# Moving the block loads and weight stores of an output projection from SyncE's queue to ScalarE's

## The reference

```
x = x + attention1(xn) + feed_forward1(xn)
# the end of attention1
out = out.transpose(0, 2, 1, 3).reshape(b, s, NH * HD)     # 2048 wide
return out @ o_w.T                                          # 2048 -> 512
# the start of feed_forward1: weights in packed 4-bit floats
nib = w[:, :, None] >> shifts & jnp.uint32(15)
vals = _FP4_LUT[nib.astype(jnp.int32)].reshape(out_f, in_p * 8)
s_full = jnp.repeat(s, group_size, axis=1)
return vals * s_full
```

## Time and profile before

| | |
|---|---|
| median of 3 runs | 2429.59 us |
| the profiled execution | 2425.01 us |
| its span, first to last instruction | 2422.9 us |
| mean granted TensorE clock | 0.96 |
| PE, PEld, DVE busy | 88%, 61%, 62% |
| ACT, POOL busy | 37%, 21% |
| DMA moved in the span | 242.99 MB |

### The profile page before, as it was taken

How to read it: one execution, slowest core, us unless ns; L and a number is a source line. 1 busy time by engine, 2 the same in 40 slices (tenths; PEclk the granted TensorE clock), 3 DMA queues, 4 the chain that set the end, 5 groups by cost and what they waited for, 6 DMA issues and landing times. The chain is left out here.

```text
span 2422.9 us, 53839 instructions
## 1 busy us (share of the span) xinstructions
PE 2127.0 (88%) x22256; PEld 1484.4 (61%) x22256; DVE 1499.6 (62%) x2380; ACT 891.2 (37%) x1858; POOL 511.2 (21%) x419
## 2 busy tenths in 40 slices
PE   4899969999996999868888988888986788799997
PEld 3677747777775788724444444444444666687776
DVE  4544323333324455468999889988894786177776
ACT  3322123222222300035656556565563232134443
POOL 0110112122220145401111111111112455221111
PEclk9999989999998999979999999999998898899999
DMA  4121144000005633233443334333342866541100
GB/s 153 71 88 36 71 154 144 17 26 17 9 0 212 198 126 122 106 83 83 104 109 90 98 81 112 102 89 98 81 119 85 262 210 194 178 144 52 53 1 35
DMA packets 183984, 242.99 MB, mean 100 GB/s; under 512 B 37744, under 2 KB 110768, under 8 KB 181072
## 3 DMA queue, kind: packets, MB, share of 16 engines
q1 hardware_dynamic: 182896, 239.59, 32.1%
q10 hardware_dynamic: 864, 0.21, 0.0%
HBM read 156.82 MB, written 82.90 MB: 99 GB/s over the span
## 5 line engine op out<-in xcount | busy, mean ns | idle before, releaser
L1479 ACT ACTIVATE a_prob<-ps,a_nmax 128x256 f32<-128x256 f32 (+7 forms) x512 | 377.4, 739 | 349.1 <-DVE a_nmax L1507 212.2
L1592 PE MATMUL ps<-a_kt,a_q 64*128 64x512 f32 (+5 forms) x1536 | 378.0, 533 | 88.0 <-ACT a_prob L1479 64.7
L1507 DVE TENSOR_REDUCE a_nmax<-ps 128x1 f32<-128x1024 f32 (+3 forms) x256 | 256.3, 1001 | 74.1 <-PE ps L1592 72.7
L1524 DVE STREAM_TRANSPOSE a_pt_long<-a_prob 128x512 f32<-128x512 f32 (+3 forms) x512 | 278.3, 582 | 0.0
L1592 PEld LDWEIGHTS ps<-a_kt,a_q 64*128 64x128 f32 x1536 | 142.0, 191 | 186.4 <-ACT a_prob L1479 117.1
L1606 PE MATMUL ps<-a_pt_long,a_v 32*64 32x256 f32 (+3 forms) x7808 | 228.0, 344 | 1.8 <-DVE a_pt_long L1524 0.2
L1991 DVE SCALAR_TENSOR_TENSOR f_part<-ps,f_gu_scale,f_part 128x512 f32<-128x512 f32 x264 | 184.7, 745 | 65.0 <-PE ps L2039 51.7
L1606 PEld LDWEIGHTS ps<-a_pt_long,a_v 32*64 32x64 f32 x7808 | 153.6, 131 | 103.4 <-issue 75.6
L1559 POOL TENSOR_TENSOR a_o<-a_left 128x256 f32<-128x256 f32 x128 | 90.4, 729 | 594.9 <-ACT a_left L1489 594.9
L2039 PE MATMUL ps<-f_xt_hi,f_gu 128*128 128x512 f32 x352 | 142.3, 404 | 22.1 <-DMA f_wd_lo<-scratch_wd 12.6
L843 POOL TENSOR_TENSOR f_hT_lo<-f_h,f_hT_hi 128x512 fp32r<-128x512 f32 x64 | 82.0, 1293 | 325.0 <-ACT f_hT_hi L826 325.0
(11 more groups left out here) (225 smaller groups left out, 4518.5 us busy)
## 6 DMA issues: line engine op xcount, KB each, us to landing
a_q<-scratch_QT SPq DMA_DIRECT2D x512, 64.0 KB, 2.1
scratch_QT<-k_qo SPq DMA_DIRECT2D x64, 256.0 KB, 2.3
a_v<-scratch_V SPq DMA_DIRECT2D x64, 256.0 KB, 4.7
scratch_OT<-a_o SPq DMA_DIRECT2D x32, 512.0 KB, 3.3
o_of<-scratch_OT SPq DMA_DIRECT2D x32, 512.0 KB, 5.5
o_packed<-in_packed SPq DMA_DIRECT2D x11, 768.0 KB, 6.8
f_xt_hi<-scratch_xt SPq DMA_DIRECT2D x8, 1024.0 KB, 7.3
f_xt_lo<-scratch_xt SPq DMA_DIRECT2D x8, 1024.0 KB, 9.1
```

Of the source, the lines that this page charges most:

```text
L1479: last = nc.scalar.activation(prob[:, n % PRING, s].rearrange("p (a w) -> p a w", w=w), SC[n % 2][:, a, 0:w], ACT.Exp, bias=nmax[:, n % 4, ...
L1507: nc.vector.tensor_reduce(nmax[:, n % 4, 0:1], SC[n % 2][:, :, 0:width(0, t)], AX.XY, ALU.max, negate=True).then_inc(maxed, 1)
L1524: last = nc.vector.transpose(pt[hf][:, lo:hi, h, t - FIRST[hf], :], src.rearrange("p (j k) -> p j k", k=32))
L1592: last = pe.matmul(sc[:, a, 0:w], q[r, slot, heads[a * hf], :], kt[r, b, keys], start=not masked, stop=True, skip_group_check=True)
```

## The change

SP keeps the loads of `stage`, `of`, `xsum` and the shift table. The block loads and all stores are issued by ACT. ACT loads the first two blocks ahead of its loop. At `STORE_AT[m]`, which is one step later than before for ACT and for POOL, it converts block m, issues the load of block m+2, stores the low down weights of block m-1 and stores the converted parts of block m. The load's wait for unpacking goes, since `convert(m)` has waited for the same block already.

```diff
-        LOAD_AT = [0, 1] + [OPS * (m - 1) // SHARE + 1 for m in range(2, NBK)]
-        STORE_AT = [OPS * (m + 1) // SHARE + 1 for m in range(NBK)]
+        STORE_AT = [OPS * (m + 1) // SHARE + 2 for m in range(NBK)]
...
             @block.sync
             def _(sp):
-                def load_block(m):
-                    if m >= 2:
-                        sp.wait_ge(unpacked, OPS * (m - 1))
-                    sp.dma_start(packed[:, m % 2, :], d["packed"][m, :, :].unsqueeze(1).broadcast_to([P // 8, 8, WC])
-                                 ).then_inc(p_in[m % 2], 16)
-                    sp.dma_start(scale[:, m % 2, :], d["down_scale"][m, :].partition_broadcast(P)
-                                 ).then_inc(p_in[m % 2], 16)
-
-                def store_block(m):
-                    sp.wait_ge(converted, 2 * m + 2)
-                    sp.dma_start(d["gu"][m], gu[:, m % 2, :].bitcast(F32)).then_inc(w_stored[m % 2], 16)
-                    sp.dma_start(d["wd"][0, m], wd[0][:, m % 2, :].bitcast(F32)).then_inc(w_stored[m % 2], 16)
-                    sp.wait_ge(down_low, m + 1)
-                    sp.dma_start(d["wd"][1, m], wd[1][:, m % 2, :].bitcast(F32)).then_inc(w_stored[m % 2], 16)
...
-                        for m in block_at(n):
-                            load_block(m)
...
-                    for m in range(NBK):
-                        if n == STORE_AT[m]:
-                            store_block(m)
...
             @block.scalar
             def _(act):
+                def load_block(m):
+                    act.dma_start(packed[:, m % 2, :], d["packed"][m, :, :].unsqueeze(1).broadcast_to([P // 8, 8, WC])
+                                  ).then_inc(p_in[m % 2], 16)
+                    act.dma_start(scale[:, m % 2, :], d["down_scale"][m, :].partition_broadcast(P)
+                                  ).then_inc(p_in[m % 2], 16)
+
+                def store_converted(m):
+                    act.wait_ge(converted, 2 * m + 2)
+                    act.dma_start(d["gu"][m], gu[:, m % 2, :].bitcast(F32)).then_inc(w_stored[m % 2], 16)
+                    act.dma_start(d["wd"][0, m], wd[0][:, m % 2, :].bitcast(F32)).then_inc(w_stored[m % 2], 16)
+
+                def store_low(m):
+                    act.wait_ge(down_low, m + 1)
+                    act.dma_start(d["wd"][1, m], wd[1][:, m % 2, :].bitcast(F32)).then_inc(w_stored[m % 2], 16)
...
+                for m in range(2):
+                    load_block(m)
                 for n in range(NSTEP + 1):
...
                         if n == STORE_AT[m]:
                             convert(m)
+                            if m + 2 < NBK:
+                                load_block(m + 2)
+                            if m:
+                                store_low(m - 1)
+                            store_converted(m)
+                store_low(NBK - 1)
```

More of the change, by code:

```diff
@@ L1689, in finished @@
             return n + 1 + (n + 1) // NK * (TT - 1)
-        def block_at(n):
-            return [m for m in range(NBK) if n == LOAD_AT[m]]
         SHARE = 3
-        LOAD_AT = [0, 1] + [OPS * (m - 1) // SHARE + 1 for m in range(2, NBK)]
-        STORE_AT = [OPS * (m + 1) // SHARE + 1 for m in range(NBK)]
+        STORE_AT = [OPS * (m + 1) // SHARE + 2 for m in range(NBK)]
         with nc.Block() as block:
```

## The result

The changed kernel took 2406.45 us (median of 4 runs, 2400.58 to 2408.3) beside 2430.39 us for the kernel before (4 runs, 2426.3 to 2431.31). The ratio is 0.9897, with a 95% interval of 0.988 to 0.9915: 24 us less, 1.0%. Timed once more beside other variants it took 2404.88 us, ratio 0.99 (0.9883 to 0.9916). The forecast was 2406.6.

The account below looks back on a forecast made before the run. SP's DMA queue, 131 us in semaphore waits with slice loads behind it, was taken to leave holes in PE, VectorE being next. Second half 13.8 plus first half 9.2 gave 23 us: 2406.6 us, range 2391 to 2426.

Parts of the forecast that it names:

- the rivals' times: Only second half gains 2415.6 us (chance 0.22); everything fits 2394 (0.15); no change 2429.6 (0.10); slower 2440 (0.08).
- SP's order: SP's DMA queue: block loads and stores leave it, and 131 us of waits that held up slice loads go.
- SP's issues and the later step: SP's saved issuing, 25 us, only in the no-change rival (0.10); conversion one step later: no gain by itself.
- Second half, 13.8 us: Tokens n = 16 to 31: PE sets the pace, 101.8 becomes 87.0 us, gain 14.8, less 1 for ACT's convert waits.
- First half, 13.1 less 3.9: Tokens n = 0 to 15: PE starts step 15 13.1 us earlier, less 3.9 for crowded DMA engines; net 9.2.
- The new wait for packed blocks: First half, VectorE waits for blocks 2, 4 and 5, now issued by ACT: 3.6 + 3.8 + 2.1 = 9.5 us.
- The adds, taken as free: VectorE's eight adds at the half, 5.0 us, counted ahead of unpacking block 7, with no wait of PE for them.
- The start: Stage start: packed(0) beside of(0) may start PE up to 2.5 us later; taken as 0, since VectorE ends the half.
- ACT's issues: Block loads and stores on ACT, up to 30 us over 11 blocks: just hidden in PE's 5.44 us step; taken as 0.
- the 3 us to spare: Second half, convert(7) on ACT: oT_lo(21) ends at 24.2 us into the half, PE needs it at 27.2.
- DMA share: First half: the DMA engines' share rises from 0.79 to 0.85 or more; 0.88 by the count.
- The upper bound: Best case, packed at 5.7 us to landing and no crowding: first half gains 22, second 14.8, 37 us in all.

Follow-up runs that it names:

- the four tests here: Changed kernel with only loads on ACT: 2425.74 us; only stores on ACT: 2412.5; all DMAs on ACT, SP's waits kept: 2425.19; kernel before with later step: 2443.27.
- the fourth: Kernel before with only conversion, low part and stores one step later, everything on SP: 2443.27 us, ratio 1.0066.

## Why the prediction was right

The mechanism was right: SP's waits, with the slices queued behind them, held PE, and with them gone VectorE bounds the first half. None of the rivals' times came. That the total agreed so closely (24 us measured, 23 forecast) is in part luck. In the traces the two halves gained 8.1 and 12.0 us, 20.1 in all; the other 4 us of the medians lie in no stage that the traces single out. And inside the first half errors of opposite sign cancelled. The terms, one by one:

- *SP's order.* Right, and shown: the waits put back, without the DMAs, cost 19 of the 24 us.
- *SP's issues and the later step, both taken as nothing.* They were not: 18 us for the DMAs' move with the waits kept, and 13 us lost by the later step while all is in SP's order. The sum holds because these two nearly cancel.
- *Second half, 13.8 us.* In the traces PE's part from step 16 on fell from 101.8 to 89.8: 12.0. The run is free of holes, as forecast. The 2 us that are missing are its slow beginning. Behind the wait for the adds step 16 took 7.98 us (1990.09 to 1998.07) and not 5.44, with a granted clock of 0.56 between 1990 and 1996 us, and I had put no restart there.
- *First half, 13.1 less 3.9.* PE reached step 16 8.1 us earlier, counted from the stage's start, against 9.2. Near as that is, every part was off. At step 15 PE was 13.0 us earlier (1979.74 - 1867.73 against 1990.9 - 1865.87), 3.8 more than forecast. The new wait for packed blocks, put at 9.5 us and 3.9 more for crowding, was 2.8: 10.6 too much. VectorE's operations, left at their old durations, took 6.1 us more: its last wo_lo ended 108.2 us after its first one began, of which 8.2 was waiting, so 100.0 us for the work that took 118.4 - 5.0 - 19.5 = 93.9 before. The rest of the difference, 0.6, is a later start.
- *The adds, taken as free.* They were not: step 15's three operations took 9.7 us and not 5, so the adds began late and PE stood 4.6 us. With it the 13.0 us at step 15 became the 8.1 at step 16.
- *Why the packed wait was small.* I counted oT_hi and both conversions, 2.8 us, as lying ahead of the load's issue, because they stand ahead of it in ACT's order. The trace shows that they don't (below). The other part is that VectorE's steps were 6.8 us long, and so it came to the block later than my 6.1 us said.
- *The start.* PE's first matmul came 3.5 us later in the stage, more than my bound of 2.5. Nothing speaks against taking 0 for its effect: made 3.1 us earlier again, the stage was 212.8 us as before, and with 2.5 operations a step 202.2 against 201.5. But in both VectorE's loads moved too, so it isn't shown by itself.
- *ACT's issues.* Hidden, as forecast: PE doesn't wait for ACT or POOL behind step 16. ACT does stand at the conversions of blocks 6 to 10, 24.1 us in all and at most 8.1 (block 6), and the 3 us to spare held.
- *DMA share.* Forecast at 0.85 or more, 0.82 measured; it was no bound. Between 1900 and 1940 us, where the residual is loaded too, it is 1.01, and VectorE's single wait for `scale` falls in there.
- *The signs named beforehand.* Three came: SP waits for w_low and o_low alone, VectorE never waits for wo_hi inside the stage, PE's second half is one run (89.8 us, a little over the 87 to 89). Two didn't: the wait for packed or scale, 2.8 us and not 5 to 15, and the DMA share.
- *The upper bound is mis-summed.* With packed at 5.7 us to landing, each of the three waits of 3.6, 3.8 and 2.1 us is 1.1 shorter. That leaves 6.2, so the first half would gain 22.6 - 6.2 = 16.4 and not 22, and the sum is 31 us and not 37.

## What to carry to other kernels

SP's queue of DMA issues behaved as an engine that works in order: a store that waited for a computation held each prefetch behind it. So the waits of the issuing queue are the view to read when loads arrive late while the DMA engines have room; a test that moves the DMAs but keeps the waits tells the two apart. It should change nothing else: the later step, a cost of 13 us in SP's order, stands in three of the four tests here, and only the fourth measures it. When such a bound goes, look at the engine next in line with the durations that it will have when it no longer pauses: here it was VectorE, 6 us slower than by its old rows. Giving it half an operation less a step in the first half (2397 us against 2405 and 2406) was worth 8 to 9 us, about a third of the change again.

## What the runs showed of the hardware that was not expected

**ACT issues a DMA while its earlier activations are still to come.** ACT's timeline in the changed kernel, at step 11. In program order the two conversions stand between oT_hi and the load:

```profile
1946.45 1.07 ACT L1750 ACTIVATE o_oT_hi<-o_of 128x1024 fp32r<-128x1024 f32 x1 [1.32 <-DMA o_of<-scratch_OT]
1946.57 0.57 ACTq L1718 DMA_DIRECT2D o_packed<-in_packed  x1
...
1947.42 1.05 ACT L1736 ACTIVATE o_gu<-o_val 128x1024 fp32r<-128x1024 f32 x1
...
1949.01 0.33 ACTq L1725 DMA_DIRECT2D scratch_gu<-o_gu  x1
```

The load went out at 1946.57, 0.12 us after oT_hi began and 0.85 us before the first conversion did. The store, which waits on the conversions' semaphore, went out behind them at 1949.01. At block 6 the conversion itself had to wait for VectorE, and the load behind it went out only when that wait ended:

```profile
1994.77 1.06 ACT L1736 ACTIVATE o_gu<-o_val 128x1024 fp32r<-128x1024 f32 x1 [8.10 <-DVE o_val L1805]
1994.77 0.55 ACTq L1718 DMA_DIRECT2D o_packed<-in_packed  x1
```

In these rows what holds a DMA in ACT's order is a semaphore that it or something ahead of it waits for, and not the work ahead.

**A VectorE operation is held while POOL works.** VectorE and POOL in the changed kernel:

```profile
1914.81 0.96 DVE L1796 TENSOR_SCALAR o_val<-o_mag 128x1536 f32<-128x1536 f32 x1
1915.80 3.96 DVE L1798 SCALAR_TENSOR_TENSOR o_val<-o_mag,o_val 128x1536 f32<-128x1536 f32 x1
```

```profile
1915.76 2.39 POOL L1766 TENSOR_TENSOR o_oT_lo<-o_of,o_oT_hi 128x1024 fp32r<-128x1024 f32 x1 [6.82 <-ACT o_oT_hi L1750]
```

The operation takes 1.76 us elsewhere; this one began 0.04 us behind POOL's and took 2.2 us more. The same holds for the whole stage. VectorE has 93 operations in it besides the adds. In the changed kernel 56 of them overlap one of POOL's in time, and 37 of these take over 0.3 us more than such an operation takes elsewhere, 66.0 us more in sum; of the 37 that overlap none, not one does. Before, 40 overlapped, 24 of them longer, by 42.2 us. That accounts for the 21.7 us more in the seven lines (and 2.1 in wo_lo), and taking 22 us of POOL's work away gave 15.6 back. That more of POOL's operations fall on VectorE's because VectorE pauses less is likely, but not shown. The Trainium skill (Trainium Architecture — The Big Picture, "What this means for kernel authors") calls the port that these two share an exclusive lock; the trace agrees, with 3.96 us in place of 1.76.

**The stages ahead differ by up to 10 us from trace to trace**, with the same instructions in them. A change of a few microseconds in one stage is better read from that stage's own length; but that is one execution: the changed kernel's two traces gave 212.8 and 212.5 us, and for no other kernel is there a second trace to say how far the length itself varies.
